# Routing of a mixture of experts: the last quarter's logits from the first layer, the choice of experts by halves

## The reference

```python
# conditioned block: second layer is W2 (192 columns, shared) and We[id of the batch] (64 columns)
h = gelu(x @ W1 + b1)                                # 1024 hidden
c = concatenate([h @ W2 + b2, h @ We[id] + be[id]])  # 256
# mixture of experts on c, 2048 rows, E = 8, top 2, CAPACITY = 512
logits = c @ Wg                                      # 2048 x 8
probs = softmax(logits); vals, idx = top_k(probs, 2)
w = vals / (sum(vals) + 1e-09)
# for k = 0, 1: place of a row in its expert = running count over the rows; kept if below CAPACITY
for e in range(8):
    out += combine[:, e] * (gelu(c @ W1[e] + b1[e]) @ W2[e] + b2[e])
```

## Time and profile before

| what | us |
|---|---|
| median of 3 runs | 1906.95 (1906.34 to 1907.31) |
| the profiled execution | 1898.26 |
| its span | 1896.5 |
| PE busy in it | 1777.5 (94%) |
| DVE busy | 1075.3 (57%) |
| ACT busy | 922.1 (49%) |
| POOL busy | 556.4 (29%) |

### The profile page before, as it was taken

One profiled execution on the slowest core, in us unless ns is written; L12 is line 12 of the kernel. 1 busy time (PEld: TensorE's weight loads), 2 busy tenths in 40 slices (PEclk: granted clock), 3 DMA queues, 4 the chain that ended last, 5 costly groups with the idle time before them and its releaser, 6 DMA issues.

```text
span 1896.5 us, 40919 instructions
## 1 busy us (share of the span) xinstructions
PE 1777.5 (94%) x16954; PEld 1284.4 (68%) x16954; DVE 1075.3 (57%) x2305; ACT 922.1 (49%) x1692; POOL 556.4 (29%) x958
## 2 busy tenths in 40 slices
PE   5999899977999969999999999999999999999997
PEld 3466768663756645777777777765777777777775
DVE  4584644135243136988888888864555554445454
ACT  2314132202243214888888888873555544445522
POOL 1362130004131063212121212103555554445413
PEclk9979899987999989999999999999999999999998
DMA  5100000402354369631101301000000000010001
GB/s 163 26 15 10 4 1 1 139 22 67 106 167 130 111 183 173 142 56 34 36 26 32 106 21 41 21 2 23 2 2 2 2 2 2 2 30 2 2 1 45
DMA packets 89323, 92.48 MB, mean 49 GB/s; under 512 B 34914, under 2 KB 74786, under 8 KB 88994
## 3 DMA queue, kind: packets, MB, share of 16 engines
q1 hardware_dynamic: 82882, 78.07, 15.2%
q0 software_dynamic: 3456, 9.44, 1.9%
q10 hardware_dynamic: 2800, 2.34, 0.4%
HBM read 67.29 MB, written 23.07 MB: 48 GB/s over the span
## 4 chain that ended last, share of the span: by engine, by line
PE 88%; DVE 5%; DMA 2%; ACT 2%; POOL 1%; issue 1%; ACTq 0%; POOLq 0%; DVEq 0%
PE PS L1696 13%; PE PS L1163 8%; PE PS L1154 7%; PE PS L1710 7%; PE PS L2035 6%; PE PS L1687 6%; PE PS L2113 5%; PE PS L2090 4%; PE PS L2040 3%; PE PS L2074 3%; PE PS L569 3%; PE PS L641 2%; PE PS L2120 2%; PE PS L648 1%; PE PS L2152 1%; PE PS L513 1%
## 5 line engine op out<-in xcount | busy, mean ns | idle before, releaser
L1869 DVE CUSTOM_DVE_ANT_0 arena<-PS,arena 128x1024 f32<-128x1024 f32 x256 | 312.0, 1219 | 63.0 <-PE PS L1687 59.0
L1790 ACT ACTIVATE arena<-arena 128x1024 f32<-128x1024 f32 x256 | 296.7, 1159 | 9.5 <-DVE arena L1869 9.1
L1696 PE MATMUL PS<-arena 128*128 128x128 f32 x2048 | 278.3, 278 | 3.1 <-issue 2.5
L1696 PEld LDWEIGHTS PS<-arena 128*128 128x128 f32 x2048 | 229.1, 142 | 63.1 <-issue 29.7
L2317 POOL TENSOR_SCALAR arena<-arena 128x384 f32<-128x384 f32 (+1 forms) x256 | 143.0, 570 | 252.0 <-DVE arena L2226 251.9
L2198 ACT ACTIVATE arena<-arena 128x385 f32<-128x385 f32 (+1 forms) x256 | 151.4, 593 | 128.6 <-DVE arena L2235 128.6
L1786 ACT COPY arena<-PS 128x512 f32<-128x512 f32 x298 | 170.0, 585 | 62.4 <-PE PS L1696 59.8
L1687 PE MATMUL PS<-arena 96*128 96x512 bf16 x512 | 154.2, 382 | 4.9 <-DVE arena L1869 3.8
L2235 DVE CUSTOM_DVE_ANT_0 arena<-PS,arena 128x384 f32<-128x384 f32 (+1 forms) x256 | 123.2, 538 | 52.3 <-PE PS L2077 39.9
L1154 PE MATMUL PS<-arena 128*128 128x512 f32 x320 | 142.5, 603 | 6.6 <-ACT arena L1256 6.6
L1876 DVE COPY arena<-PS 128x512 f32<-128x512 f32 x214 | 146.9, 686 | 2.0 <-PE PS L1696 1.8
(11 more groups left out here) (319 smaller groups left out, 3131.3 us busy)
## 6 DMA issues: line engine op xcount, KB each, us to landing
arena<-in_L_ffn_W SPq DMA_DIRECT2D x16, 1024.0 KB, 7.4
arena<-prior SPq DMA_DIRECT2D x16, 512.0 KB, 4.2
parts<-arena SPq DMA_DIRECT2D x24, 256.0 KB, 5.4
arena<-parts SPq DMA_DIRECT2D x96, 64.0 KB, 3.0
arena<-parts SPq DMA_DIRECT2D x48, 128.0 KB, 9.6
prior<-arena SPq DMA_DIRECT2D x4, 1024.0 KB, 6.5
ye<-arena SPq DMA_DIRECT2D x7, 512.0 KB, 3.0
ya<-arena SPq DMA_DIRECT2D x7, 512.0 KB, 4.8
```

Of the source, the lines that this page charges most:

```text
L1696: h = e.transpose(PS[:, i, P * j:P * j + P], Sb[z % 3][:, 512 * g + P * j:512 * g + P * j + P], ident)
L1790: e.activation(Sb[z % 3], Sb[z % 3], ACT.Exp, bias=mr[:, z % 4:z % 4 + 1], scale=-1.0).then_inc(s_exp, 1)
L1869: e.tensor_tensor_reduce(Sb[z % 3], ps, Ab[m % 2], 1.0, 3e38, ALU.add, ALU.min, mr[:, z % 4:z % 4 + 1]).then_inc(s_ttr, 1)
```

## The change

- *A new step G in `phase_b`*, between the last `x` and `d1` of batch 0: PE multiplies the turned second layer (`WcT`, 256 by 1024, of batch 1's expert part) with `Wg`, eight times two products of eight columns, and two products of a matrix of ones with `Wgb`, which is `Wg` scaled by the second layer's bias. DVE copies the 72 columns to `WcG`. POOL makes `Wgb` at the head of its part of the stage. Seven loads are added at the head of SP's part, in front of `W1c`; the turned weights come from the host's layout as inputs.
- *The last quarter's logits* come from `hb` and `WcG` (`gate`: four tiles by eight products of eight columns), and DVE adds the bias' part at the copy. `cT` 3 and `logits` 3 are gone.
- *The order*: `COND` has `gate` 3 ahead of `logits` 2, and the last quarter's second layer is cut into its four tiles (`co3`, one group each): tile 0 after `co` 2, tile 1 after `logits` 2, tiles 2 and 3 between `places` and `slots`. `places` and `slots` are in the list.
- *The choice by halves*: DVE chooses for the first 1024 rows after `logits` 1 and for the others after `logits` 2 (`select`).
- *After the places*: the first product of `hi2` goes to ACT, the second to POOL, each after `hi1`. DVE makes `lo1` for k = 0 right after `hi1`, then evicts tiles 2 and 3 of `co3`, then makes `lo1` for k = 1. The one-hot rows (`hi1`, `hi2`, `lo1`) now lie in the other half of `hbs`, which `ch` 3 does not use. SP stores the last quarter after tile 3.

```diff
@@ phase_b
+    Wgb = arena.up(16).rearrange("p (c n) -> p c n", c=2)
+    WcT = top0[:, 0:2 * FH].rearrange("p (c f) -> p c f", c=2)
+    WcG = K.WcG = st[0][:, 418:490]
+    bcT = st[0][:, 490:492]
...
-    ORDER = project(0) + [("mx", 1)] + in_turn(pairs(0), project(1)) + in_turn(first[:11], split[:3])
+    ORDER = project(0)[:5] + [("G", 1)] + project(0)[5:] + [("mx", 1)] + in_turn(pairs(0), project(1)) + in_turn(first[:11], split[:3])
...
     def sp(e, w):
+        r = e.value_load(K.ids[0:1, 3:4], min_val=0, max_val=E - 1)
+        e.dma_start(K.Wg, kmaj(a["L0_ffn_Wg"])).then_inc(s_wt, 16)
+        e.dma_start(bcT[:, 0:1], a["L0_cond2_b2"][0:128].rearrange("(p o) -> p o", o=1)).then_inc(s_wt, 16)
+        e.dma_start(bcT[0:64, 1:2], a["L0_cond2_b2"][128:192].rearrange("(p o) -> p o", o=1)).then_inc(s_wt, 16)
+        e.dma_start(bcT[64:128, 1:2], a["L0_cond2_be"][bass.ds(r, 1)].rearrange("e (p o) -> (e p) o", o=1)).then_inc(s_wt, 16)
+        e.dma_start(WcT[:, 0, :], a["L0_cond2_W2T"][0:128, :]).then_inc(s_wt, 16)
+        e.dma_start(WcT[0:64, 1, :], a["L0_cond2_W2T"][128:192, :]).then_inc(s_wt, 16)
+        e.dma_start(WcT[64:128, 1, :], a["L0_cond2_WeT"][bass.ds(r, 1)].rearrange("e p f -> (e p) f")).then_inc(s_wt, 16)
         e.dma_start(K.W1c, kmaj(a["L0_cond2_W1"])).then_inc(s_wc[0], 16)
-        e.dma_start(K.Wg, kmaj(a["L0_ffn_Wg"])).then_inc(s_wc[0], 16)
...
+        def gate():
+            i = group("G")
+            w.wait_ge(s_wt, 112)
+            for f in range(8):
+                for k in range(2):
+                    e.matmul(PS[:, i, 8 * f:8 * f + 8], WcT[:, k, P * f:P * f + P], K.Wg[:, k, :], start=k == 0, stop=k == 1)
+            w.wait_ge(s_wgb, 2)
+            for k in range(2):
+                h = e.matmul(PS[:, i, 64:72], K.onesm, Wgb[:, k, :], start=k == 0, stop=k == 1)
+            h.then_inc(ring.sem, 1)
...
+                e.tensor_copy(WcG, PS[:, group("G"), 0:72]).then_inc(ring.into("G"), 1)
...
     def pool(e, w, own):
+        w.wait_ge(s_wt, 112)
+        for k in range(2):
+            e.tensor_scalar(Wgb[:, k, :], K.Wg[:, k, :], bcT[:, k:k + 1], 1.0, ALU.mult, ALU.mult).then_inc(s_wgb, 1)
@@ phase_d
-    COND = [("ch", 2), ("cT", 0), ("cT", 1), ("ch", 3), ("logits", 0), ("logits", 1), ("co", 2), ("cT", 2), ("co", 3), ("logits", 2), ("cT", 3), ("logits", 3)]
+    COND = [("ch", 2), ("cT", 0), ("cT", 1), ("ch", 3), ("logits", 0), ("logits", 1), ("co", 2), ("co3", 0), ("cT", 2), ("gate", 3), ("logits", 2), ("co3", 1), ("places", 0), ("co3", 2), ("co3", 3), ("slots", 0)]
...
+        def gate(q):
+            i = group(("logits", q))
+            for t in range(4):
+                for f in range(8):
+                    w.wait_ge(*ring.emptied(("ch", q, f)))
+                    h = e.matmul(PS[:, i, 8 * t:8 * t + 8], hb[q % 2][:, f, P * t:P * t + P], K.WcG[:, 8 * f:8 * f + 8], start=f == 0, stop=f == 7)
+            h.then_inc(ring.sem, 1)
+
+        def result3(t):
+            i = group(("co", 3, t))
+            for f in range(8):
+                h = e.matmul(PS[:, i, 0:D], hb[1][:, f, P * t:P * t + P], Wc[1][:, f, :], start=f == 0, stop=f == 7)
+            h.then_inc(ring.sem, 1)
...
-        w.wait_ge(s_top, 1)
+        w.wait_ge(s_top, 2)
         e.activation(EX, LG, ACT.Exp).then_inc(s_pexp, 1)
+        w.wait_ge(s_hi, 1)
+        e.activation(hi2[:, :, 0, :], hi1, ACT.Identity, scale=kslot[:, 8:9]).then_inc(s_hi_p, 1)
...
+        def select(t0, t1):
...
+        def result3(t):
+            key = ("co", 3, t)
+            e.tensor_tensor(C1[1][:, 4 + t, :], PS[:, group(key), 0:D], bc[1], ALU.add).then_inc(ring.into(key), 1)
...
+                if q:
+                    w.wait_ge(*ring.emptied(key))
+                    select(4 * q - 4 if q == 1 else 8, 8 * q)
...
         e.tensor_tensor(hi1, ioh.unsqueeze(1).broadcast_to([P, 32, 32]), hk, ALU.is_equal).then_inc(s_hi, 1)
-        w.wait_ge(s_hi, 1)
-        e.tensor_scalar(hi2[:, :, 0, :], hi1, kslot[:, 8:9], None, ALU.mult).then_inc(s_hi, 1)
         for k in range(2):
+            e.tensor_tensor(lo1[:, k], io1.unsqueeze(1).broadcast_to([P, 16, P]), lo_[:, k, :].unsqueeze(2).broadcast_to([P, 16, P]), ALU.is_equal).then_inc(s_lo, 1)
             if k == 0:
-                t128 = kslot[:, 25:41].unsqueeze(1).unsqueeze(3).broadcast_to([P, 2, 16, 32])
-                e.tensor_tensor(hi2[:, :, 1, :].rearrange("p (k t) j -> p k t j", k=2), hi1.rearrange("p (k t) j -> p k t j", k=2), t128, ALU.mult).then_inc(s_hi, 1)
-            e.tensor_tensor(lo1[:, k], io1.unsqueeze(1).broadcast_to([P, 16, P]), lo_[:, k, :].unsqueeze(2).broadcast_to([P, 16, P]), ALU.is_equal).then_inc(s_lo, 1)
+                for t in (2, 3):
+                    result3(t)
...
+        t128 = kslot[:, 25:41].unsqueeze(1).unsqueeze(3).broadcast_to([P, 2, 16, 32])
+        w.wait_ge(s_hi, 1)
+        e.tensor_tensor(hi2[:, :, 1, :].rearrange("p (k t) j -> p k t j", k=2), hi1.rearrange("p (k t) j -> p k t j", k=2), t128, ALU.mult).then_inc(s_hi_t, 1)
```

More of the change, by code:

```diff
@@ L680, in pe @@
                 result(b, *s)
+            elif name == "G":
+                gate()
             elif name == "u":
@@ L1027, in phase_d @@
             plan_out("co", q)
-        else:
-            ring.plan(("logits", q), "dve")
-    ring.plan("places", "dve")
-    ring.plan("slots", "dve")
+        elif name == "co3":
+            ring.plan(("co", 3, q), "dve")
+        elif name in ("logits", "gate"):
+            ring.plan(("logits", q), "dve")
+        else:
+            ring.plan(name, "dve")
     EARLY = 3
@@ L1051, in phase_d @@
         K.sem("d_" + n) for n in ("b2", "iota", "pk", "rows", "bits", "onet", "onep", "form", "log", "diff", "lb", "pmask"))
[L1052 to L1053 removed]
+    s_top, s_pexp, s_oh, s_lo, s_hi, s_hi_p, s_hi_t, s_gi, s_comb = (
+        K.sem("d_" + n) for n in ("top", "pexp", "oh", "lo", "hi", "hi_place", "hi_tile", "gi", "combine"))
     s_w1 = [K.sem(f"d_w1_{j}") for j in range(2)]
@@ L1215, in pe @@
                 result("co", q, hb[q % 2], Wc[1])
-            else:
-                logits(q)
-        places()
-        slots()
+            elif name == "co3":
+                w.wait_ge(*ring.emptied(("ch", 3, 7)))
+                result3(q)
+            elif name == "gate":
+                gate(q)
+            elif name == "logits":
+                logits(q)
+            elif name == "places":
+                places()
+            else:
+                slots()
         for q in range(E + 1):
@@ L1321, in dve @@
             elif name == "co":
-                result("co", q, bc[1], C1[1][:, 4 * (q % 2):4 * (q % 2) + 4, :])
+                result("co", q, bc[1], C1[1][:, 0:4, :])
+            elif name == "co3" and q < 2:
+                result3(q)
+            elif name == "gate":
+                key = ("logits", q)
+                e.tensor_tensor(v8(LG[:, 32 * q:32 * q + 32]), v8(PS[:, group(key), 0:32]), K.WcG[:, 64:72].unsqueeze(1).broadcast_to([P, 4, 8]), ALU.add).then_inc(ring.into(key), 1)
             elif name == "logits":
```

65 lines of the change are left out of this document (35 added, 30 removed).

## The result

Before and after were run again in turns on one chip, 20 runs each. Before took 1903.68 us in the median (1899.74 to 1909.75), after 1910.19 us (1904.23 to 1913.61). The ratio is 1.0034, with a 95% interval of 1.0023 to 1.0045: slower by 6.5 us (4.4 to 8.6). Forecast were +5.9 us over the earlier median. The profiled execution of after took 1913.37 us (span 1911.5), so the two profiled executions lie 15 us apart, more than twice the medians. A part of the difference between the two traces is thus not the change's: before's profiled execution (1898.26) was quicker than all twenty runs, after's one of its slowest.

The account below looks back on a forecast made before the run. TensorE, with 88% of the last chain, was taken to bound the kernel. G's +6.8 us and the routing's -0.9 gave +5.9, so 1912.9 us in the median; own range 1909.5 to 1916, wider range 1904 to 1917.

Parts of the forecast that it names:

- G's own cost: First stage, ahead of `d1`: 36 thin instructions at half clock take 8.1 us, `d1`'s second half starts at 76.7, +6.8 us.
- Rival B: Step G: clock rises within G, or fillers and `d1` run full; G costs about +2, total 1909.0 us; chance 0.14.
- Behind it PE is dense to 98 us ... nothing off PE is late there that could swallow it: Stretch after `d1`: DVE and POOL work from PE's output, so G's whole +6.8 us passes on.
- Loads: Seven DMAs on SP's queue ahead of W1c, which is first read some 200 us later: cost 0.
- Gate: Last quarter's logits in the routing: 64 instructions, about 22 at full clock (2.5 us), 42 at half (9.4), to 406.3.
- rival A: G and gate: thin products do not lower the clock, gate takes 7.4 us; net -6.8, 1900.1 us; chance 0.14.
- Logits, co3(1), choice, places: Routing behind the gate: third quarter's logits 3.6 us, co3(1) 6.1, choice's second half 3.1, places 1.2, done at 417.2.
- hi2 on ACT and POOL: After the places: 0.49 + 1.22 us off DVE, POOL's product delays second `lo1`; gather gains 0.9 us, 2.1 without delay.
- The store: Fourth store of rows: issued at 424.7, lands at 427.6, two us before the indices; hidden, costs from 5 us landing.
- rival D: Store of rows lands after 8 us or more, gather up to 5 us later; net about +10, 1917; chance 0.05.
- Rival C: Last co3 tiles: clock not back, co3(2) and co3(3) take 14.7 us; net +13.4, 1920.4 us; chance 0.05.
- The sum: Whole kernel: +6.8 us for G, -0.9 at the gather, together +5.9 us, 1912.9 us.

Follow-up runs that it names:

- y_filled: After with four more unread 512-column products in PE's wait ahead of the first group of `y` products: 1895.43 us, ratio 0.9993 to before.
- g_only: After's first stage (with G) and before's routing, G's result not read: 1913.42 us, ratio 1.0054 to before.
- hi_dve: After with G ahead of `yn(0,0)`, first quarter's logits between halves of `ch` 3, second `hi2` product back on DVE: 1889.22 us, ratio 0.996 to before.
- woven: `g_moved` with each thin product of the gate set behind a wide one of co2: 1899.84 us, ratio 0.9967 to before.
- g_again: The kernel `g_only` unchanged, profiled once more: 1910.37 us in one run.
- g_moved: After with G moved to just ahead of `yn(0,0)`, its weights in another buffer and loaded later: 1894.94 us, ratio 0.9965 to before.
- shift_small: Before with 22 unread 512-column products ahead of `d1`'s first half, without G: 1905.7 us, ratio 1.0015 to before.
- route_only: Before's first stage and after's routing, other numbers loaded in place of G's result: 1899.05 us, ratio 0.9987 to before.
- shift_wide: Before with 38 unread 512-column products ahead of `d1`'s first half, without G: 1909.26 us, ratio 1.0031 to before.
- no_gate: Before with choice by halves, co3 by tiles and `hi2` on ACT and POOL, but neither G nor gate: 1904.84 us, ratio 1.0007 to before.

## Why the prediction was right, and where it was not

**G's own cost: right to 0.6 us.** `d1`'s second half was forecast at 76.7 and came at 76.72, with the clock at 0.50 to 75 us. But 0.7 us of that lie ahead of G (62.88 for 62.2); G took 7.8 us for 8.1, and `d1` with the fillers 6.1 for 6.4. So G itself moved its followers by 6.2 us where +6.8 was forecast (5.8 to 6.2 in the four profiles that have it there), and that the place came out to 0.02 us is luck. Rival B is refuted in its mechanism: the clock stayed at half through all of G.

**"Behind it PE is dense to 98 us ... nothing off PE is late there that could swallow it": the failed step.** True as far as it went (the next batch's first product in the chain starts at 105.13 instead of 98.21), but it looked for what could swallow the shift, not for what could add to it, and put the stretch from 98 us to the routing at nothing. In the medians G costs 10.3 us (7.4 to 13.1), some 3.5 above the forecast's 6.8. In the pair of traces that stretch cost 11.9 us: 2.8 ahead of the `y` products, whose cause is not known, and 9.1 behind, the half clock among them. PE's idle time ahead of them is 1.55 us with G and was 0.92, and `y_filled` shows that filling it takes 10.0 us off that stretch of the trace and 7.8 (6.5 + 1.3) off the median's distance to before. That the median of `g_only` shows less of it than the trace fits with before having it in some of its own executions, as `hi_dve` has it without G; no profile of before shows that.

**Loads: right.** G shows no wait for them.

**Gate: right in kind, 2 us too dear.** The clock fell, as the forecast said against rival A, in an unbroken row of products with PE busy. But it fell after 4.0 us, near 413.5, not 2.5: some 36 instructions at full and 28 at half, 9.98 us for 11.9. In the six kernels with the gate in one row it took 9.5 to 10.3 us. Rival A's mechanism is refuted here, in G and in `woven`. The Trainium skill, "TensorE: Matmul & The Clock Gate", section "Why this matters for your kernels", advises to leave no idle gaps between bursts of products; the rows of 413 and of 380 to 412 us above show a clock lost and kept down without one. At the `y` products a filled gap kept the clock, as that advice has it; but the page means longer gaps than those 1.55 us.

**Logits, co3(1), choice, places: right to 0.4 us each.** 3.4 us for the third quarter's logits, for 3.6; 5.7 for co3(1), for 6.1; the choice took 2.8 us for 3.1 and was over at 425.9, ahead of the places as forecast; the places 1.3 for 1.2. With the gate, co3(0)'s start to the places is 428.42 - 405.11 = 23.3 us, forecast 416.0 - 389.8 = 26.2.

**hi2 on ACT and POOL: mechanism right, size off.** `lo1` of k = 1 was delayed by POOL's product, but by 0.5 us of its own length rather than by a gap of 1.2 ahead of it: POOL's instruction was issued as early as 433.82 and counts 3.89 us with its wait, until 437.7. The places to the indices took 13.07 us, forecast 13.7. The Trainium skill, "SBUF — State Buffer", section "SBUF: two separate sides", has a DVE operation with two SBUF inputs and a GpSimd one that reads SBUF exclude each other for whole instructions; the trace agrees, with a second `lo1` of 2.79 us beside POOL and 2.28 in `hi_dve`.

**The store: right.** The two stores of rows in the window of the routing landed in 3.0 us in the median, and the gather waited for DVE's indices alone. That refutes rival D. Rival C is refuted by the last two tiles of co3, which ran at full clock, 32 in 7.18 us.

**The sum.** From co2's end to the indices after takes 441.49 - 405.11 = 36.4 us, before 40.8: -4.4 us where -0.9 was forecast. A further 3.5 us in the pair of traces come from the first logits and co2, which after ran at full clock and before did not the earlier trace rows; that is not the change's. So in the medians +6.8 was too small by some 3.5 us, and in the traces -0.9 was too small a gain by 3.5 (in the medians the routing gave -2.5, with -5.9 to +0.8). The two errors offset: +5.9 forecast, +6.5 measured. The time came out right by luck in that respect. The gather at 437.5 in the new trace came at 442.55, 5 us late: 11.9 us were lost between `d1` and the first logits, and from these to the gather it took 7.0 less than forecast.

**Left open:** why the clock does not fall at the turning ten us ahead of the `y` products with G ahead of `d1` and once without it, and does otherwise, which sets PE's idle time there; what the 2.8 us ahead of them are; and how often either is so in executions that were not profiled.

## To carry to other kernels

A step that is short at full clock is best placed in a wait of its engine that exists anyway: the same 36 products cost 10.3 us in the median ahead of dense work, and 0.7 us in the trace and nothing that could be told in the median ahead of `yn`. After placing it, look at PEclk in every later stretch, not only where the step stands: the forecast priced the row correctly and missed a cold stretch 130 us on, which four unread products in one wait took away again. In this kernel many thin products did best in short rows between long wide ones, better in the traces than in one long row or woven singly into the wide work.

## What the runs showed of the hardware

0.6 us more of idle time at one place went with some 10 us: in the four profiles where PE idled 1.55 us ahead of the `y` products the clock went to half for about 20 us of nearly unbroken work, in the nine with 0.92 it stayed full there. In those nine it had been at half a moment before, at the turning; in the one with 0.68 it had not, and it stayed full all the same.

A faster PE can idle longer: the turning took 1.97 us at full clock instead of 2.37 to 3.27, DVE's work behind it did not get shorter, and PE's wait for DVE grew from 0.92 to 1.55 us.

Whether 32 thin products in a row cost the clock differed between the profiles: the first logits took 3.63 us in seven of the eleven profiles that have them so (after, `g_only`, `g_again`, `g_moved`, `woven`, `shift_small`, `y_filled`) and 4.34 to 4.67 us in four (before, `route_only`, `shift_wide`, `no_gate`), and co2 behind them, where nothing is woven into it, 14.1 against some 16.5 us. In rows of 16, in three profiles, it was never lost there.

`woven` stayed at half clock for nearly 40 us with PE busy in every window shown, a product of 256 columns behind each of 8; with 256-column products alone the clock was back after 3.4 us.

Executions of one kernel on one core spread by 4.2 us (`y_filled`) to 27 us (`woven`), with the mean granted clock. Two single profiles can lie 15 us apart where the medians lie 6.5.
